# Edge lists of a graph network: 13 tiles in a row per partition, bases spread by TensorE, run flags only in the general path

## The reference

```
x = x + rgcn(layernorm(x), W0, src, dst, edge_type, edge_weight)  # per relation: sum of weight * h[src] by dst, times a block-diagonal matrix, summed over 8 relations
x = x + moe_ffn0(layernorm(x))                                     # 8 experts, top 2, gelu, layer norm
x = x + gat(layernorm(x), (src, dst), W, a_src, a_dst)             # attention over incoming edges, 8 heads, softmax by dst, sum of att * proj[src]
x = x + moe_ffn1(layernorm(x))                                     # 8 experts of three layers, softmax gate
```

## Time and profile before

| | us |
|---|---|
| median of 3 runs | 5015.17 |
| the profiled execution | 5006.31 |
| its span | 5004.5 |
| GpSimd busy | 3118.0 (62%), 3259 instructions |
| TensorE busy | 4123.0 (82%) |
| VectorE busy | 2025.7 (40%) |
| ScalarE busy | 881.1 (18%) |
| DMA | 545.86 MB, mean 109 GB/s |

### The profile page before, as it was taken

The page is one execution under the profiler, slowest core; times in us unless marked ns, Lnnn a source line. Parts: engine busy times, 40 slices in busy tenths (PEclk is TensorE's granted clock), DMA queues, the critical chain, the costliest instruction groups (busy, mean ns, idle before and its releaser), DMA issues. The chain is left out here.

```text
span 5004.5 us, 68827 instructions
## 1 busy us (share of the span) xinstructions
PE 4123.0 (82%) x18968; PEld 3226.1 (64%) x18968; DVE 2025.7 (40%) x8089; ACT 881.1 (18%) x1867; POOL 3118.0 (62%) x3259
## 2 busy tenths in 40 slices
PE   1488777877787777859888579999999999999998
PEld 0477777877777777755565236666666666666665
DVE  3445555555555555543444223233332333233321
ACT  2011111111111111113333001111111111111112
POOL 0477777777777777730000477777777777777750
PEclk9977777777777677769999689999999999999999
DMA  3444444444444444430111444444444444444430
GB/s 117 109 118 122 122 121 121 122 121 122 122 121 123 121 121 121 122 95 30 43 38 37 133 118 117 122 122 118 127 126 122 127 119 126 126 122 120 124 97 9
DMA packets 278080, 545.86 MB, mean 109 GB/s; under 512 B 72578, under 2 KB 172716, under 8 KB 276652
## 3 DMA queue, kind: packets, MB, share of 16 engines
q0 software_dynamic: 154944, 429.93, 31.0%
q1 hardware_dynamic: 76657, 65.73, 4.3%
q10 hardware_dynamic: 46301, 48.48, 3.0%
HBM read 483.03 MB, written 60.87 MB: 109 GB/s over the span
## 5 line engine op out<-in xcount | busy, mean ns | idle before, releaser
L641 POOL DMA_INDIRECT ring<-xn,index x1612 | 1529.7, 949 | 652.0 <-issue 480.7
L1531 POOL DMA_INDIRECT ring<-table,index x1616 | 1554.0, 962 | 548.7 <-issue 491.9
L756 PE MATMUL bank<-spare,ring 128*128 128x64 f32 x6448 | 1059.1, 337 | 449.9 <-DMA ring<-xn,index 407.8
L756 PEld LDWEIGHTS bank<-spare,ring 128*128 128x128 f32 x6448 | 1022.8, 250 | 476.7 <-issue 399.0
L1693 PE MATMUL bank<-ring,acc 128*128 128x264 f32 x3232 | 876.4, 408 | 129.4 <-DMA ring<-table,index 116.3
L1693 PEld LDWEIGHTS bank<-ring,acc 128*128 128x128 f32 x3232 | 597.9, 195 | 429.7 <-DMA ring<-table,index 247.8
L1871 DVE TENSOR_SCALAR acc<-iota,off 128x128 f32<-128x128 f32 x1734 | 355.7, 298 | 635.7 <-ACT off L1544 631.2
L855 DVE TENSOR_TENSOR cells<-cells,bank 128x128 f32 x812 | 233.9, 288 | 434.7 <-PE bank L756 352.5
L835 DVE TENSOR_SCALAR spare<-iota,scal 128x64 f32<-128x64 f32 x1612 | 404.8, 334 | 2.9
L1709 PE MATMUL bank<-acc,wa 128*128 (+1 forms) x832 | 380.5, 601 | 26.5 <-ACT ework L1579 26.5
L1734 PE MATMUL bank<-wo,ework 128*128 128x256 f32 x1664 | 381.6, 383 | 1.8 <-DVE y L1942 1.8
(11 more groups left out here) (269 smaller groups left out, 3241.5 us busy)
## 6 DMA issues: line engine op xcount, KB each, us to landing
ring<-table,index POOLq DMA_INDIRECT x1616, 2.8
ring<-xn,index POOLq DMA_INDIRECT x1612, 2.8
sums<-acc ACTq DMA_DIRECT2D x101, 132.0 KB
sums<-spare ACTq DMA_DIRECT2D x101, 128.0 KB
acc<-sums ACTq DMA_DIRECT2D x13, 528.0 KB
y<-x SPq DMA_DIRECT2D x13, 512.0 KB
table<-frow SPq DMA_DIRECT2D x48, 132.0 KB
nsums<-sums ACTq DMA_DIRECT2D x49, 128.0 KB
```

The lines of the kernel that those rows point to most:

```text
L641: pool.indirect_dma_start(ring[:, m * BT + t, :], None, k.xn_d, bass.IndirectOffsetOnAxis(ap=index[m][:, t:t + 1], axis=0)).then_inc(got[m ...
L756: ins = pe.matmul(win[q][:, t, h * CELLS:(h + 1) * CELLS], ring[:, m * BT + q * QUAD + t, h * P:(h + 1) * P], onehot[:, q * QUAD + t, :], ...
L1531: pool.indirect_dma_start(ring[:, par * BT + t, :], None, k.table1_d, bass.IndirectOffsetOnAxis(ap=index[par][:, t:t + 1], axis=0)).then_i ...
```

## The change

- Each partition holds 13 tiles in a row: partition q holds edges 1664 q to 1664 q + 1663, so a contiguous run is 6,656 B. A list is loaded in three pieces: partitions 0 to 95, 96 to 122 and the 1578 edges that remain. SP issues the first piece at once; GpSimd's memsets now touch partitions 96 to 127 of all 1664 columns, and the second piece waits for the memset of its list. `dst` has a semaphore of its own.
- Turned blocks come out with every 13th tile, so they are kept with a step of 13 columns (`by_tile`). VectorE keeps `off_t` and `rel_t`; ScalarE keeps `k.src` and the weights, each with PSUM banks and semaphores of its own.
- ScalarE casts `src` and `rel`, when all lists are there.
- VectorE writes each base 128 times in a row (`base_all`), and 13 matmuls with the identity give the bases as a row on all partitions; ScalarE keeps them as `base_row`, in the space of `dst_f`. `k.base16` is made from it. The bases still go to DRAM once, for the general path.
- x: chunks 0, 2 and 4 are loaded from ACT's queue, 1 and 3 from GpSimd's.
- The zeros go out on SP's queue; they and `wblk` stand before the five stores of x.
- `starts`, `ends`, `both` and the 13 loads of `prev` leave this block. The general path of `gnn1_ffn1` makes them from a load of its own.
- VectorE's order: `spread` and `scale` of the chunks lie between the steps of the tables; chunk 3 comes after the weights' sums and chunk 4 after the flag.

```diff
-        def flat(ap):
-            return ap.rearrange("(k q e) -> q k e", q=P, e=P)
...
+        def loads(t, arr):
+            flat = t[:].rearrange("p b e -> p (b e)")
+            by_part = arr[0:whole * WIDE].rearrange("(q e) -> q e", e=WIDE)
+            return [(flat[0:SPLIT, :], by_part[0:SPLIT, :]), (flat[SPLIT:whole, :], by_part[SPLIT:whole, :]),
+                    (flat[whole:whole + 1, 0:rest], arr[whole * WIDE:E].rearrange("(q e) -> q e", e=rest))]
+        def by_tile(held):
+            return held.rearrange("p (q b) -> p b q", b=BLOCKS)
         @block.gpsimd
+            for t, v in ((dst_i, PAD_NODE), (src_i, 0), (rel_i, 0), (weight, 0.0)):
+                pool.memset(t[SPLIT:P, :, :], v).then_inc(filled, 1)
...
+            for c in (1, 3):
+                pool.dma_start(x[:, chunk(c), :], by_parts(g["x"])[:, chunk(c), :]).then_inc(xloads[c], 16)
         @block.sync
-            sp.wait_ge(filled, 11)
-                for dst, src in loads:
-                    sp.dma_start(dst, src).then_inc(loaded, 16)
+            for n, (t, name) in enumerate(arrays):
+                for i, (dst, src) in enumerate(loads(t, g[name])):
+                    if i == 1:
+                        sp.wait_ge(filled, n + 1)
+                    sp.dma_start(dst, src).then_inc(loaded if n else dst_loaded, 16)
...
+            sp.wait_ge(based, 1)
+            sp.dma_start(k.base_d.rearrange("(q k) -> q k", k=BLOCKS), base_c[:]).then_inc(stored, 16)
+            sp.wait_ge(filled, 6)
+            for r in range(0, AHEAD, P):
+                n = min(P, AHEAD - r)
+                sp.dma_start(k.x2_all[r:r + n, :], zeros[:n, 0:D]).then_inc(padded, 16)
+                sp.dma_start(k.sums_d[r:r + n, :], zeros[:n, :]).then_inc(padded, 16)
+            sp.dma_start(k.sums0_d[0:AHEAD0, :], zeros[:AHEAD0, 0:D]).then_inc(padded, 16)
             w = g["L0_gnn_weight"].rearrange("r (b i o) -> b i r o", i=32, o=32)
             for b in range(D // 32):
                 q = 32 * (b % 4)
                 sp.dma_start(k.wblk[q:q + 32, b // 4, :, q:q + 32], w[b]).then_inc(k.wload, 16)
+            for c in range(CHUNKS_X):
+                sp.wait_ge(x_made, c + 1)
+                sp.dma_start(by_parts(k.xn_d)[:, chunk(c), :], x[:, chunk(c), :]).then_inc(x_stored, 16)
         @block.scalar
+            act.wait_ge(loaded, 16 * 9)
+            act.copy(src_f[:], src_i[:]).then_inc(cast, 1)
+            act.copy(rel_f[:], rel_i[:]).then_inc(cast, 1)
...
+            root(0)
+            act.wait_ge(offset, 1)
+            for u in range(4):
+                m = min(4, BLOCKS - 4 * u)
+                act.wait_ge(rows_made, u + 1)
+                act.copy(by_tile(base_row)[:, 4 * u:4 * u + m, :], rows_ps[:, u, 0:m, :]).then_inc(rows_kept, 1)
+            normalise(0)
+            root(1)
+            keep(0, k.src[:])
+            normalise(1)
+            root(2)
+            keep(1, k.meta[:, WEIGHT_KIND, :])
+            normalise(2)
+            for c in (3, 4):
+                root(c)
                 normalise(c)
```

More of the change, by code:

```diff
@@ L435, in _, with keep @@
-            st.then(dve.tensor_scalar(ends[:], ends[:], -BIG, None, ALU.mult))
-            st.then(dve.tensor_tensor(both[:], ends[:, :, 0], ends[:, :, 1], ALU.add))
-            dve.sem_inc(ready, 1)
+            def keep(i, held):
+                for u in range(4):
+                    b, m = 4 * u, min(4, BLOCKS - 4 * u)
+                    dve.wait_ge(turn_v, 4 * i + u + 1)
+                    st.then(dve.tensor_copy(by_tile(held)[:, b:b + m, :], turned_v[:, u % 2, 0:m, :]))
+                    dve.sem_inc(taken_v, 1)
@@ new lines, in _ @@
+            spread(0)
+            scale(0)
+            keep(0, off_t[:])
+            spread(1)
+            scale(1)
+            keep(1, rel_t[:])
+            dve.wait_ge(rows_kept, 4)
+            bases = base_row.rearrange("p (b t) -> p b t", t=BT)
+            st.done(dve.tensor_scalar(k.base16[:], bases[0:1, :, 0], 0.0, float(COLS - P), ALU.max, ALU.min))
+            dve.wait_ge(turn_v, 8)
+            st.then(dve.tensor_tensor(shift.rearrange("p (b t) -> p b t", t=BT), bases,
+                                      bases[:, :, 0:1].broadcast_to([P, TPAD // BT, BT]), ALU.subtract))
@@ new lines, in _ @@
+            spread(2)
+            scale(2)
+            dve.wait_ge(filled, 8)
+            st.done(dve.tensor_copy(due[:], due_i[:]))
+            st.done(dve.tensor_copy(part[:], part_i[:]))
+            st.done(dve.memset(k.offs[:, 0, CARRY:SPAN], 0.0))
+            st.done(dve.tensor_reduce(wide[:], off_t[:], AX, ALU.max))
+            st.then(dve.tensor_tensor(step[:, 1:], bases[:, 1:, 0], bases[:, 0:TPAD // BT - 1, 0], ALU.subtract))
+            st.done(dve.tensor_scalar(k.offs[:, 1:, CARRY], step[:, 1:], -1.0, part[:], ALU.mult, ALU.add))
@@ L439, in _ @@
+            st.done(dve.tensor_scalar(k.base[:], shift[0:1, :], 0.0, float(P), ALU.max, ALU.min))
+            dve.wait_ge(taken_s, 4)
+            st.then(dve.tensor_tensor(near, off_t[:], shift, ALU.add))
+            st.then(dve.tensor_reduce(far[:], near, AX, ALU.max))
+            st.then(dve.scalar_tensor_tensor(far[:], wide[:], float(P // NEAR), far[:], ALU.mult, ALU.max))
+            dve.sem_inc(far_made, 1)
             dve.wait_ge(w_loaded, 32)
@@ L1653, in general @@
             def general():
+                act.wait_ge(e_filled, 4)
+                with nc.allow_non_contiguous_dma(reason="one destination per tile"):
+                    for dst, src in edge_loads():
+                        act.dma_start(dst, src).then_inc(e_loaded, 16)
+                    act.wait_ge(e_ready, 7)
+                    act.dma_start(k.starts_d.rearrange("(k q) e -> q k e", q=P), e_starts).then_inc(e_stored, 16)
+                    act.dma_start(k.ends_d.rearrange("(k q) e -> q k e", q=P), e_ends).then_inc(e_stored, 16)
+                    act.dma_start(k.both_d.rearrange("(k q) -> q k", q=P), e_both).then_inc(e_stored, 16)
+                act.wait_ge(e_stored, 48)
                 act.sem_inc(p_done, 2)
```

242 lines of the change are left out of this document (105 added, 137 removed).

## The result

The changed kernel takes 4976.51 us (median of 4 runs, 4974.1 to 4977.46) against 5017.17 for the kernel before in the same comparison: 40.7 us less, ratio 0.9914 (95% interval 0.9895 to 0.9933). Forecast were 4956.5 and 58.7 us less. The sign and the place are right; the gain is 18 us short.

A forecast was written before the change was run, and what follows sets the result against it. It took five DMA engines carrying x to bound the changed table block, which delays the gather loop: 102.1 us of terms, begun at 5.2 plus 2.1 landing, end 109.4; 58.7 less from 5015.17 gives 4956.5, range 4938 to 4980.

The forecast's parts named there:

- rival 3: Table block's loading: lists still late, or a share on one engine (+24 us); 4981, or 4968 for late lists alone; chance 0.08.
- the sum on five engines: Table block's DMA: x loads and stores, lists, zeros, `wblk` and small items total 102.1 us on the five engines carrying x.
- 109.4: Forecast end of the table block in us, instead of 168.1: 58.7 us less.
- cover: Table block: stores ready before the five engines are free for them, by 13 us at the end, hiding compute work.
- That the block's length goes straight into the time: Second block, before the gather loop: ending N us earlier moves the kernel's end by N us.
- The lists at 34: Table block's loading: all edge lists landed at 34 us instead of 74.5, taking turns with x's rows and GpSimd's chunks.
- GpSimd's chunks at 6.1 us: Two x chunks loaded from GpSimd's queue: spread evenly over 16 engines, they cost each 160 KB, 6.1 us.
- Rival 2: Table block's x loads: GpSimd's queue gives no more engines, +13.4 us, block end 122.8, kernel 4970; chance 0.17.
- the 6.0 us for `wblk`: `wblk` loads on SP's queue: 128 pieces of 128 B per engine at 47 ns each, 6.0 us.
- The chain's 51 us from lists to the last chunk: VectorE's and ScalarE's work in the table block: from lists at 34 to ScalarE's last normalising at about 85.
- Rival 4: Table block's strided writes over 5 x 1664 columns: kernel slower, 5027 at 10 ns per column; chance 0.02.
- Flags, `prev`, casts and copies taken from VectorE: "worth nothing beyond the chain": Table block: work removed from VectorE, such as casts (2.0 us) and copies (4.8), gains nothing beyond the compute chain.

The follow-up runs named there:

- split_all: Changed kernel with each x chunk loaded and stored in two pieces, of 112 and 13 partitions, on the same queues: 4965.6 us, ratio 0.9895 to the kernel before.
- split_stores: Changed kernel with only the x stores in two pieces of 112 and 13 partitions: 4968.5 us, ratio 0.9902 to the kernel before.
- one_queue: Changed kernel with all five x chunks loaded from ScalarE's queue, none from GpSimd's: 4975.4 us, ratio 0.9912 to the kernel before.
- pieces_512: Changed kernel with the same list layout, but each list's rows loaded as 512 B pieces: 4994.3 us, ratio 0.9949 to the kernel before.
- before_split_2: Kernel before with only x loaded and stored in pieces of 112 and 13 partitions, a repeat on another chip: 4965.3 us against 5007.9.
- x0_first: Changed kernel, x in 112 and 13 partitions, chunk 0 issued at once, the other chunks when the lists have landed: 4949.5 us against 5007.9 before.
- cut_120: As x0_first, with pieces of 120 and 5 partitions for x, 120 and 3 for the lists: 4957.2 us, ratio 0.9895 to the kernel before.
- lists_first: Changed kernel with all x loads of both queues issued only when the lists have landed: 6330.2 us against 6377.5 before on a slow chip.
- lists_first_128: As lists_first, x loaded on 128 partitions with 48 rows each, input misplaced, only load rates to be read: x at 424 GB/s, no time given.
- lists_first_split: As lists_first, with x loaded and stored in pieces of 112 and 13 partitions: 6304.0 us against 6377.5 before on a slow chip.
- ordered_split: Changed kernel, x in 112 and 13 partitions, ScalarE's queue only, behind the lists, chunks 0 and 1 before the casts: 6324.9 us against 6392.5 before.

## Why the prediction came out as it did

The measured 4976.5 lies in the stated range, near its upper end, but not by the path that was forecast. The block went as in rival 3, to which the prediction gave 0.08: its sign, ScalarE's first cast after 50 us, is there at 57.2. The range holds it because it was drawn out to rival 3, not because the sum on five engines was right. By the prediction's own terms the 17.9 us between 109.4 and 127.3 are 23.2 for lists later than 34, less 12.6 of cover (109.4 - 96.8), plus 4.6 for a longer chain and 2.7 for a store that was still under way behind it.

*That the block's length goes straight into the time: right.* Over eight versions on chips like the first the block's end and the time moved together: 40.8 and 40.7 us (the change), 52.9 and 53.6 (split_all), 48.8 and 50.7 (split_stores), 41.4 and 43.8 (one_queue), 28.3 and 24.9 (pieces_512), 44.9 and 42.6 (before_split_2), 63.3 and 58.4 (x0_first). cut_120 is the loosest, 60.3 and 50.7, where the interval of the ratio is some 7 us to either side.

*The lists at 34: wrong, 57.2. This is the step that failed*, the term "36 x (9.7/25 + 0.25)", with 5.5 us more for GpSimd's turns. It took 0.25 us for a list row and 0.39 for a row of x, the rate of an engine when only five are active. The queues of the changed kernel (packets, MB, share of 16 engines), 4 to 12 us, then 20 to 28 us, then ScalarE's queue (q10) from 36 to 44 us:

```profile
q1 hardware_dynamic: 217, 1.28, 65.8%
q10 hardware_dynamic: 35, 0.36, 18.9%
```

```profile
q0 software_dynamic: 130, 1.19, 74.5%
q1 hardware_dynamic: 70, 0.30, 17.5%
q10 hardware_dynamic: 19, 0.19, 11.7%
```

```profile
q10 hardware_dynamic: 40, 0.36, 11.5%
```

A packet of SP's queue (q1) occupies an engine for 65.8% x 16 x 8 / 217 = 0.39 us, one of GpSimd's (q0) 74.5% x 16 x 8 / 130 = 0.73 us, and a row of x on ScalarE's queue by the same sum 0.69 us at first and 0.79 then: 1.6 to 2 times my figures. From 36 to 44 us, when all queues together fill only 37% of the engines, it is 0.37 again. So on the five engines a list row in turn with both other queues costs some 1.8 us, where the sum had 0.64. The earlier trace rows had a hint of it: 206 GB/s at a share of 0.81 are 15.9 GB/s for a busy engine, not 26.3. one_queue shows the part of GpSimd's turns (13.7 us of the 23), lists_first that of all x (34 us), and lists_first_128 against lists_first_split that a packet of x is cheaper in the layout on 128 partitions (0.35 us of an engine against 0.55, ScalarE's queue, 28 to 40 us). Why the others cost twice as much stays open.

*GpSimd's chunks at 6.1 us, spread over 16: right in the spread, wrong in the price.* The share of 74.5% can't be five engines. Rival 2's mechanism (no more engines) did not come true, but its advice did: taken back, the time stays (4975.4 against 4976.5). The rule of the Trainium skill that the prediction weighed ("DMA: Bandwidth & Descriptors", rules for kernel authors), that spreading DMAs over SP, ACT and GpSimd doesn't help, speaks for that, and the two runs agree.

*The sum of 102.1 on five engines as the bound: wrong in this kernel.* It would bind with lists at 34; since the chain came 23 us later, the engines were idle in part (share 0.25 from 92 to 108), and the chain became the bound. The block ends at 104.5 (chunk 3 normalised, 99.50 + 5.02) + 2 x 9.7 + about 3. It is rival 3 in mechanism. Its number for lists 24 us late was 121 and 4968: 6 us short, since the chain ended 3.8 us after its 109 and chunk 3's store was not through then (2.7). In one_queue the sum does bind. One of its terms was too large: the 6.0 us for `wblk` take the spacing of the packets in the earlier trace rows for their price, and the share of 30.8% there makes 14 ns a packet, not 47. In the changed kernel these loads (65 to 70 us, 2016 packets, 46.6% of the engines) took 18 ns each, 2.4 us of an engine.

*The chain's 51 us from lists to the last chunk: 55.6 measured* (57.2 to 112.8). The largest part that the prediction did not have is a wait of 2.8 us: VectorE waits for TensorE to turn `rel`, and TensorE does it behind the blocks of `src`, for which it waits until ScalarE has kept the first ones. The strided copies were dearer too. Order of time and groups of the changed kernel, in answer to the earlier trace rows:

```profile
73.20 3.99 DVE L414 COPY rel_t<-turned_v 128x512 f32<-128x512 f32 x4 [2.79 <-PE turned_v L488]
...
L414 DVE COPY off_t<-turned_v 128x512 f32<-128x512 f32 x3 | 3.2, 1051 | 0.4
...
L358 ACT COPY src_of<-turned_s 128x512 f32<-128x512 f32 x3 | 3.0, 1055 | 0.3 <-PE turned_s L488 0.3
```

1051 and 1055 ns for 512 columns, against 692 and 592 without the step: 0.7 and 0.9 ns per column, above the 0.6 that the earlier trace rows suggested, and 7 us over five arrays on the two engines. How much of that lies on the chain no run shows. Rival 4's mechanism is there at a tenth of its price (its "4.6 us per 512 columns" is a slip: 10 ns more per column are 5.1 us more).

*The 13 us of cover* were used up by the late lists, so the strided copies, and every us on the chain, now count; the prediction had said so for that case.

*Flags, `prev`, casts and copies taken from VectorE: "worth nothing beyond the chain". That held only for a chain with cover.* Here the chain is the bound, so they count. With x cut in both, VectorE needs 67.0 us from the lists to its last operation in the old kernel (50.7 to 117.7, before_split_2) and 54.9 in the changed one (52.6 to 107.5, split_all), and the block ends 8 us earlier. No run takes them out one by one. The tail after VectorE's last operation fell from 26.5 to 15.3 us (127.33 - 112.06), but not because `starts_d` is gone and the zeros and `wblk` moved: before_split_2 has all of them in their old places and a tail of 5.5 us. It was x's stores on five engines that held the queue.

Not tried: moving the zeros and `wblk` back behind the stores, so what their new place costs or gains isn't measured.

## What to carry to other kernels

Look at the DMA share and the rate before the layout of the data: a share of 0.31 with a kernel waiting for loads means that few engines carry them. On SyncE's and ScalarE's queues the number of partitions decided how many (125 went to five, 112 and 13 filled all sixteen). Cutting 125 partitions into 112 and 13 did as much as rewriting the whole table stage. A share of 1.00 isn't the full rate either: the same share went with 206 and with 424 GB/s. Where several queues are in flight, ask whose packet a small one waits for, and give the first thing needed the engines alone; and don't price a transfer among sixteen busy engines by the rate of five.

## What the runs showed that was not expected

Sixteen engines all busy with loads moved 206 to 246 GB/s into 96, 112 or 120 partitions (with the rest in a second piece) and 424 into 128; five engines into 125 partitions did 26 GB/s each, six tenths of the sixteen's total with a third of the engines. A store from 112 and 13 partitions ran at 305 GB/s for 4 us (split_all, 64 to 68).

Chips differ far more than these kernels do: two of them took 6377 and 6392 us for the kernel that takes 5008 to 5019 on others. There GpSimd waits for ScalarE's next indices in the first gather loop (300 to 1800 us, ordered_split), a wait that the changed kernel's trace has not:

```profile
POOL ring L651 <- ACT index L664: 458.2, 53, 10.2
```

TensorE's granted clock, a mean between its levels of 1.2 and 2.4 GHz, was 0.65 on such a chip (lists_first_split) and 0.71 in the changed kernel's trace from 200 to 2100 us. That is 8% less, while GpSimd got through 1072 instructions there instead of 1515 in the same stretch, 29% fewer. What makes these chips slower stays open.
